# Writing the Toeplitz matrices of a long convolution out in HBM before they are loaded

## What is computed

```python
x = x + layernorm(hyena(layernorm(x)))     # first layer
x = x + layernorm(ffn(layernorm(x)))       # second layer: W1, gelu, W2, with a small per-batch addition
# hyena, the part that matters here:
z = rmsnorm(u, pre_norm_w) @ in_proj_w.T                  # 768 channels, then a causal conv of 3 taps
x2, x1, v = split(z_pre, 3)
h = sum(residues[:, :, None] * exp(log_poles * t), axis=1)  # a filter per channel, 16 poles, 4096 taps
xv = x1 * v
y = (causal_conv(xv, h) + xv * D_skip) * x2               # 4096 taps, by FFT in the reference
y = y @ out_proj_w.T + u                                  # then rmsnorm, a gated MLP of 672, residual
```

## Time and profile before

| | us |
|---|---|
| median of 3 runs | 1122.17 (1121.68 to 1126.74) |
| the profiled execution | 1130.82 |
| its span | 1129.1 |
| busy in it: PE, DVE, ACT, POOL | 1058.1, 880.7, 724.5, 295.2 |
| moved by DMA | 89.23 MB, 79 GB/s over the span |

### The profile page before, as it was taken

The page is one execution under the profiler, slowest core; times in us unless marked ns, Lnnn a source line. Parts: engine busy times, 40 slices in busy tenths (PEclk is TensorE's granted clock), DMA queues, the critical chain, the costliest instruction groups (busy, mean ns, idle before and its releaser), DMA issues.

```text
span 1129.1 us, 25540 instructions
## 1 busy us (share of the span) xinstructions
PE 1058.1 (94%) x9280; PEld 1026.8 (91%) x9280; DVE 880.7 (78%) x2313; ACT 724.5 (64%) x1607; POOL 295.2 (26%) x560
## 2 busy tenths in 40 slices
PE   4999999798678999999999999988999999999996
PEld 4899998576568999999999999988999999999996
DVE  7998998654368788888778888788778888877774
ACT  6888887555455666666666666565666566666553
POOL 6677674630010112111112111111111211111121
PEclk9999999889688999999999999998999999999999
DMA  3333321997743233443333344452333333333000
GB/s 123 114 122 118 108 75 39 273 252 196 136 78 66 38 57 48 51 56 66 57 57 48 49 53 65 90 123 38 59 55 57 49 49 52 56 62 57 26 14 29
DMA packets 108926, 89.23 MB, mean 79 GB/s; under 512 B 7121, under 2 KB 103537, under 8 KB 108545
## 3 DMA queue, kind: packets, MB, share of 16 engines
q1 hardware_dynamic: 107632, 85.16, 36.8%
q0 software_dynamic: 672, 2.39, 0.6%
q10 hardware_dynamic: 496, 0.05, 0.0%
HBM read 62.12 MB, written 17.07 MB: 70 GB/s over the span
## 4 chain that ended last, share of the span: by engine, by line
PE 66%; DVE 6%; DMA 4%; issue 3%; ACT 1%; POOL 1%; ACTq 0%; SPq 0%; DVEq 0%; POOLq 0%
PE ps_ring L1393 35%; PE ps_w L1393 14%; PE ps_m L1393 9%; PE ps_o L1393 3%; DMA toep<-taps_scratch 3%; PE ps_rt L1403 2%; PE ps_y L823 2%; PE ps_y L832 1%; DVE base L1249 1%; POOL sc L1017 1%; PE ps_m L1439 1%; DVE bn L1155 1%; PE ps_s L801 0%; DVE prod L1197 0%; DVE pt_l L1167 0%
## 5 line engine op out<-in xcount | busy, mean ns | idle before, releaser
L1017 POOL TENSOR_TENSOR sc<-sc,neg_half 128x2 f32<-128x2 f32 x128 | 95.5, 746 | 738.4 <-DVE sc L1348 449.7
L1077 ACT ACTIVATE gate<-ps_ring 128x256 f32<-128x256 f32 x192 | 73.2, 382 | 137.3 <-PE ps_ring L1393 136.2
L1393 PE MATMUL ps_ring<-mt_h,wl_h 128*128 128x256 f32 x640 | 130.6, 287 | 6.4 <-ACT mt_h L1144 6.4
L1393 PE MATMUL ps_ring<-mt_l,wl_h 128*128 128x256 f32 x640 | 130.3, 286 | 6.4 <-DVE mt_l L1167 6.4
L1098 ACT ACTIVATE hid<-ps_ring,b1s 128x256 f32<-128x256 f32 x256 | 114.0, 491 | 31.7 <-PE ps_w L1393 13.9
L1393 PE MATMUL ps_ring<-mt_h,wl_l 128*128 128x256 f32 x640 | 130.1, 286 | 0.0
L1167 DVE TENSOR_TENSOR ht_l<-hid,ht_h 128x256 fp32r<-128x256 f32 x256 | 103.2, 423 | 15.4 <-ACT ht_h L1102 9.5
L1393 PEld LDWEIGHTS ps_ring<-mt_h,wl_h 128*128 128x128 f32 x640 | 101.5, 196 | 7.7 <-ACT mt_h L1144 4.4
L1393 PEld LDWEIGHTS ps_ring<-mt_l,wl_h 128*128 128x128 f32 x640 | 101.3, 196 | 7.6 <-DVE mt_l L1167 7.6
L1393 PE MATMUL ps_ring<-xt_h,we_h 128*128 128x256 f32 x512 | 102.6, 282 | 2.3 <-DVE prod L1197 1.5
L1197 DVE TENSOR_TENSOR prod<-ps_ring,gate 128x256 f32<-128x256 f32 x192 | 80.9, 421 | 29.6 <-ACT gate L1077 25.7
(11 more groups left out here) (179 smaller groups left out, 2772.2 us busy)
## 6 DMA issues: line engine op xcount, KB each, us to landing
toep<-taps_scratch SPq DMA_DIRECT2D x30, 512.0 KB, 4.9
xa<-in_x SPq DMA_DIRECT2D x16, 512.0 KB, 4.5
x_scratch<-x2c SPq DMA_DIRECT2D x16, 512.0 KB, 3.5
x2s<-x_scratch SPq DMA_DIRECT2D x32, 256.0 KB, 6.9
xa_c<-in_x SPq DMA_DIRECT2D x32, 256.0 KB, 2.7
xb_c<-in_x SPq DMA_DIRECT2D x32, 256.0 KB, 2.7
out<-frow SPq DMA_DIRECT2D x32, 256.0 KB, 2.9
yin<-seq SPq DMA_DIRECT2D x124, 64.0 KB, 6.2
```

The source lines that it names most:

```text
L1017: nc.gpsimd.tensor_tensor(sc[:, to], sc[:, to], neg_half[:, 0, 0:CC], ALU.pow).then_inc(S[done], 1)
L1077: nc.scalar.activation(gate[rows_of, m % 2], ring[m % RING][rows_of, 0], ACT.Gelu_apprx_tanh).then_inc(S["gate_done"], 1)
L1393: mm = nc.tensor.matmul(out, lhs(a, kk), rhs(b, kk), start=(j == 0), stop=(closed and j == len(todo) - 1))
```

## The change

A new tensor toep_dram (toep_scratch in the trace) in HBM takes the 30 groups that are not loaded early, 15.7 MB, as (30, 128, 8, 128): each partition's 8 rows stand behind each other, 4 KB. From unit 6 to unit 15 of the first stage SP issues three DMAs per unit that read toeplitz_rows(taps_dram, g) and write toep_dram, HBM to HBM. In the scan stage load(g) reads toep_dram, and SP waits once, ahead of the first load, until all 30 are written.

```diff
+    toep_dram = nc.dram_tensor("toep_scratch", (GROUPS - TOEPS_EARLY, P, GC, CH), F32, kind="Internal").ap()
...
+            toep_written = sem(early, "toep_written")
...
+        def matrices_at(u):
+
+            steps_left, count = UA - LAST_POWERS - 3, GROUPS - TOEPS_EARLY
+            i = u - LAST_POWERS - 3
+            return range(TOEPS_EARLY + i * count // steps_left, TOEPS_EARLY + (i + 1) * count // steps_left)
...
                     for g in range(TOEPS_EARLY):
                         sp.dma_start(toep_early(v, g), toeplitz_rows(taps_dram, g)).then_inc(v["toep_early_in"], 16)
+                if u > LAST_POWERS + 2:
+                    for g in matrices_at(u):
+                        sp.dma_start(v["toep_dram"][g - TOEPS_EARLY], toeplitz_rows(taps_dram, g)
+                                     ).then_inc(v["toep_written"], 16)
...
-                sp.dma_start(toep[:, k % TOEPS], toeplitz_rows(taps_dram, g)).then_inc(toep_in[k % TOEPS], 16)
-
+                sp.dma_start(toep[:, k % TOEPS], v["toep_dram"][k]).then_inc(toep_in[k % TOEPS], 16)
+
+            sp.wait_ge(v["toep_written"], 16 * (GROUPS - TOEPS_EARLY))
             for g in range(TOEPS_EARLY, GROUPS):
                 load(g)
```

## The result

The change makes the kernel 0.6% faster: ratio to before 0.9941, 95% interval 0.9929 to 0.9954, about 6.7 us by the means of 20 runs of each. The medians are 1120.5 us against 1127.8, 7.3 apart; two of the three runs of before that were known at first are the quickest of its twenty. The direction held, the size was a little more than half.

A forecast was written before the change was run, and what follows sets the result against it. It took waits for toep loads, with DMA nearly full in the scan stage, as the bound: 14.2 us of waits less 1 and 1.5 gives 11.7, so 1122.2 - 11.7 = 1110.5 us, range 1107 to 1138 (forecast's own 1107 to 1113).

The forecast's parts named there:

- The writing out costs nothing: First stage, steps 6 to 15: thirty HBM to HBM transfers fit in idle DMA time, cost 0.
- I take 1.9 to 2.3: First stage: us per HBM to HBM transfer, between bounds of 1.9 and 3.8; three counted as 6 us.
- the free 7.6 us: First stage: DMA time left in an 11 us step after xa and the x2 store take 3.4 us.
- 201.8: Scan stage start: time in us up to which SP's wait costs nothing; group 2 needed at 205.49, quickest load 3.7.
- 14.2 us of waits: Scan stage: waits for toep loads and their slow clock, the most the change can give back there.
- The usual load lands near 3.3 us: the three late waits go: Scan stage, groups after 238.69 us: 0.5 us off each load's landing, with 5.0 available, removes 3.6 us of waits.
- lpb: load 9 is 0.6 us late: Scan stage behind lpb: 3.3 + 2.3 = 5.6 us to land against 5.0 available.
- 1.5 us for the whole place: Scan stage around lpb: loss left there, including slow stretches of POOL's work beside VectorE.
- The start: Scan stage start: load 3 in time at 206.3 us, load 5 perhaps about 1 us late beside POOL's loads.
- The second rival: Scan stage: pieces are not what is short; late waits and half the large ones stay, 5.3 us back, 1117 us; chance 0.14.
- The signs: If right: Toeplitz waits under 3 us, groups every 2.02, scan DMA share near 0.7, 11.0 us steps, first load at 199.3.
- The sign of being wrong: SP waiting for toep_written past 202 us, VectorE waiting for xa, or toep loads still landing after 4.9 us median.

The follow-up runs named there:

- e9: The change without loading lpb or POOL's out_w and l3_w (POOL's two first loads stay; output differs), timed against the kernel before: ratio 0.9909.
- e5: The change with the 1.05 MB load of lpb left out (output differs), timed against the kernel before: ratio 0.9953.
- e2: The change with toep_scratch laid out by channel, so scan-stage loads read 512-byte pieces, timed against the kernel before: ratio 1.0008.
- e3: The change with six buffers for toep loads instead of three, timed against the kernel before: ratio 0.9883.
- e6: The change with four buffers for toep loads instead of three, timed against the kernel before: ratio 0.9894.
- e4: The kernel before with six toep buffers instead of three, nothing written out, timed against the kernel before: ratio 0.9933.
- e7: The change with every matrix written a second time to a spare tensor and SP waiting for all 60, timed against the kernel before: ratio 1.0526.

## Why the prediction came out as it did

- **The writing out costs nothing: right, with less to spare than I wrote.** The step "I take 1.9 to 2.3" was low: 2.4 us per transfer, not 2.0. Three take 7.1 to 7.3 of the free 7.6 us, and the last matrix was written at 199.02, not 197.7, 0.3 us before SP's wait and 2.8 before 201.8. The 214 GB/s for copies between HBM tensors (the Trainium skill, DMA: Bandwidth & Descriptors, Latency and other measured facts) is what the runs show, 216, with rows of 512 bytes as well: the sum by that page, 2.45 us and 7.35 for three, was the better one. The discount for small rows that the prediction tried on it (154 GB/s) did not appear.
- **"14.2 us of waits" was one execution's.** The stages of before with their usual loads took 78.45, 76.53 and 74.87 us; the first is 1.8 above their mean. So some 2 us of the forecast were probably never there in the median run; from group 15 on alone the three lost 3.6, 2.1 and 1.6 us. What the change left was about 62.8 + 8.5 us in both of its profiles.
- **"The usual load lands near 3.3 us: the three late waits go": wrong, this is the step that failed.** It let the landing time fall with the bytes per second. In the traces a load's landing is told by 16 increments of its semaphore, and it has landed with the last. For the 30 toep loads, medians of each:

```
us from the issue to the        1st increment   8th    15th   last
before, 512-byte pieces             3.4          3.5    4.2    4.9
the change, 4 KB pieces             3.1          3.5    4.3    4.8
```

  The larger pieces brought only the first increments forward. The last one comes 1.3 us behind the 8th in both kernels (medians; 0.2 to 3.1 us). It is not one straggler behind fifteen that are done: the last comes more than 1 us behind the 15th in 14 of the 30 loads of before and in only 6 of the change. The increments are drawn out over the second half, and the sum had no term for that. With 5.0 us to have, a load that takes 4.8 in the median is late again and again: 12 of the change's 30 took more than 5.0. Late losses of 1.4 us (group 22), 0.4, 0.3 and 0.2 stayed where the forecast had none (1.3 in all in the second profile), and in e9, with no other traffic beside them, 1.1, 0.3 and 0.4.
- **"lpb: load 9 is 0.6 us late" and 1.5 us for the whole place: mis-sized.** It measured 4.8 us (4.4 in the second profile), slow clock with it, and this is the largest part of what the forecast missed (3.3 us). The sum started from the same 3.3 us for a load alone; with 4.8 in its place it gives 7.1 us, 2.1 late. The loads of groups 9 to 11 landed after 6.3, 8.2 and 7.2 us instead of 5.6. I had put POOL's loads aside; out_w goes out at 217.38, 0.1 us ahead of the load of group 10. (The row of 217 to 224 us from which the rate of lpb's pieces was worked out had out_w in it too.) Without lpb the waits came behind POOL's next load (e5); only with both gone did they go (e9).
- **The start: right.** Load 3 in time, 0.7 us lost at group 5, 1 forecast. Here, with three loads queued, the rate did count: they landed at 203.2, 204.5 and 208.1 us, and in before at 203.9, 210.0 and 213.0.
- **The second rival**, "landing may be a matter of latency and of one slow engine, and lpb and POOL's loads collide as before", given 0.14, was the one that came nearest in size (5.3 us, measured 6.7). That is in part luck: its heading, that the pieces are not what is short, is refuted by e2, and one slow engine is not what the increments show. What it had right is that lpb and POOL's loads still collide and that the late waits stay. I had the evidence in the earlier trace rows, 3.7 for the quickest and 4.9 for the median load of the same size, and read the difference as bandwidth.
- **The signs.** As said for a right forecast: the first load at 199.30 and steps of 11.0 us in the first stage. Not so: waits of 5.6 us, not under 3, and a DMA share of 0.79 in the scan stage, not 0.7. The sign of being wrong came nearly to the letter: loads that land after 4.8 us in the median, 4.9 was named.

What stays open: why the last increments come so late, and whether they belong to the same DMA engines each time, which the traces do not name. One more figure on it: of the change's 4 KB packets between 240 and 256 us half took 0.16 us, but one in ten 0.37 us or more, and the longest 1.2. The rest of e3's loss, VectorE's scan beside POOL's work, was seen but not tried.

The version to keep is e3 or e6: the change with four to six buffers, 12 to 13 us faster than before, where the change alone gives 6.7. The size of the pieces and the depth add up nearly in full: 6.7 us for the one, 7.6 for the other (e4), 13.2 together (e3).

## What to carry to other kernels

A load is there when the last of its 16 increments is, so measure the time a buffer gives it against the slow landings and not against bytes divided by bandwidth; where a profile shows short waits for loads at a DMA share below 1, try one more buffer before anything else. Larger pieces paid most where loads met other traffic, and rewriting data HBM to HBM in a stage with idle DMA was free as long as it fitted: count 2.4 us per 512 KB here, and know what stands behind it in the same queue. Where removing one cause of a wait brings nothing, look where the wait has gone.

## What the runs showed of the hardware

- Transfers HBM to HBM in rows of 512 bytes moved 216 GB/s (524,288 bytes in 2.4 us; e7, and the change's last step). What stands behind them in the queue waits: an x2 store behind six of them landed 8.9 us after its issue (e7), not 3.5.
- SP's issuing takes longer when its own queue holds several DMAs of 1024 pieces: 0.93 us for one when little is queued, 2.0 in the median and up to 3.9 when several such are (e7), and a whole stage's end waits for it.
- A load's 16 increments are spread out: for 512 KB the first came after 3.1 to 3.4 us, the 8th after 3.5, the last after 4.8 to 4.9 in the median, with pieces of 512 bytes and of 4 KB alike.
- A share of busy DMA near 1 did not mean that no more would fit. 512-byte loads moved 253 GB/s at a share of 0.94 with three buffers and 284 at 1.07 with six. The rate per share is nearly the same (269 and 265), but the share went past 1, so the 269 that the prediction took for the most was not the most.
